# A graph network on one core: VectorE makes all selection matrices of a tile before the layer norm of the preceding tile

## What is computed

```python
x = layernorm(x + x @ W)              # W: 256 x 256, edge weights set at (src, dst)
X = x
for l in range(4):
    h   = einsum('ni,rio->rno', X, weights[l])          # 4 relations
    msg = h[etype, src] * inv_deg[:, None]
    agg = segment_sum(msg, dst)
    out = agg + X @ roots[l] + biases[l]
    X   = elu(layernorm(out) * gamma[l] + beta[l]) + X
out = layernorm(x + X)
```

## Time and profile before

| | before |
|---|---|
| median of three executions | 2757.57 us |
| profiled execution, device time | 2755.74 us |
| its span on the core | 2754.0 us |
| mean granted clock of PE | 0.814 |
| PE busy (matmuls) | 2166.8 us, 79% |
| DVE busy | 1636.5 us, 59% |
| GpSimd busy | 1515.0 us, 55% |
| ScalarE busy | 371.2 us, 13% |
| L464 PE, aggregation matmuls (two per visit) | 3712, 1269.6 us busy |
| L276 GpSimd, gathers | 1568, 1507.3 us busy |
| L919 DVE, selection matrices | 1856, 609.8 us busy |
| L373 PE, products | 800, 419.7 us busy |

### The profile page before, as it was taken

One profiled execution on the slowest core, in us unless ns is written; L12 is line 12 of the kernel. 1 busy time (PEld: TensorE's weight loads), 2 busy tenths in 40 slices (PEclk: granted clock), 3 DMA queues, 4 the chain that ended last, 5 costly groups with the idle time before them and its releaser, 6 DMA issues.

```text
span 2754.0 us, 45427 instructions
## 1 busy us (share of the span) xinstructions
PE 2166.8 (79%) x7689; PEld 1300.0 (47%) x7690; DVE 1636.5 (59%) x5784; ACT 371.2 (13%) x765; POOL 1515.0 (55%) x1591
## 2 busy tenths in 40 slices
PE   1667976777988888788888897988888868877665
PEld 0345444666544555433445564344455534444543
DVE  3988249788544567523455674345566624457677
ACT  0554320232000111100001110000011100000000
POOL 1000033000777777477777774777777567777772
PEclk9888985899778899956789997577899965667787
DMA  4000241000334444333344442334444343334341
GB/s 154 3 0 0 107 159 42 0 0 0 105 113 128 135 143 151 105 105 105 120 127 144 143 152 90 105 113 128 127 143 149 122 143 105 105 105 120 104 121 49
DMA packets 103156, 280.46 MB, mean 102 GB/s; under 512 B 27612, under 2 KB 38986, under 8 KB 102734
## 3 DMA queue, kind: packets, MB, share of 16 engines
q0 software_dynamic: 75264, 205.62, 25.5%
q10 hardware_dynamic: 17878, 62.19, 5.9%
q1 hardware_dynamic: 9848, 10.82, 1.3%
HBM read 219.61 MB, written 58.91 MB: 101 GB/s over the span
## 4 chain that ended last, share of the span: by engine, by line
PE 44%; DVE 15%; issue 13%; DMA 10%; POOL 10%; DVEq 4%; ACT 1%; POOLq 1%; SPq 1%; ACTq 0%
PE acc L464 25%; POOL ring L276 10%; DMA ring<-h_rows,idx 9%; PE hp L373 7%; PE pw L373 6%; DVE S L896 2%; PE acc L455 2%; DVE ring L746 1%; DVE hot_s L869 1%; DVE hot_n L869 1%; PE pw L349 1%; DVE S L919 1%; PE tr L362 1%; ACT XT L499 1%; POOLq L185 1%
## 5 line engine op out<-in xcount | busy, mean ns | idle before, releaser
L276 POOL DMA_INDIRECT ring<-h_rows,idx x1568 | 1507.3, 961 | 1189.2 <-issue 906.7
L464 PE MATMUL acc<-ring,S 128*128 x3712 | 1269.6, 477 | 250.9 <-SPq L229 137.3
L464 PEld LDWEIGHTS acc<-ring,S 128*128 128x128 f32 x3712 | 752.0, 225 | 744.8 <-issue 673.9
L919 DVE TENSOR_SCALAR S<-iota,ecol 128x128 f32<-128x128 f32 x1856 | 609.8, 370 | 791.0 <-PE acc L464 696.3
L373 PE MATMUL hp<-wts,XT 128*128 (+1 forms) x416 | 215.1, 665 | 22.4 <-ACT XT L499 22.4
L373 PE MATMUL pw<-wts,XT 128*128 (+1 forms) x384 | 204.6, 682 | 20.3 <-ACT XT L499 20.3
L869 DVE TENSOR_TENSOR hot_s<-iota,place 128x400 bf16<-128x400 f32 x196 | 112.4, 574 | 99.4 <-PE acc L416 84.7
L557 ACT ACTIVATE work<-work 128x256 f32<-128x256 f32 x100 | 41.7, 417 | 942.1 <-DVE work L949 931.6
L455 PE MATMUL acc<-wts,XT 128*128 (+1 forms) x400 | 122.5, 434 | 45.9 <-issue 39.2
L373 PEld LDWEIGHTS hp<-wts,XT 128*128 128x128 f32 x416 | 84.4, 214 | 122.3 <-issue 122.3
L373 PEld LDWEIGHTS pw<-wts,XT 128*128 128x128 f32 x384 | 80.1, 220 | 116.3 <-issue 116.3
(11 more groups left out here) (213 smaller groups left out, 1398.6 us busy)
## 6 DMA issues: line engine op xcount, KB each, us to landing
h_rows<-hst ACTq DMA_DIRECT2D x100, 512.0 KB
ring<-h_rows,idx POOLq DMA_INDIRECT x1568, 2.7
wts<-weights SPq DMA_DIRECT2D x32, 128.0 KB, 2.7
x_rows<-X ACTq DMA_DIRECT2D x1, 3200.0 KB, 10.1
wts<-x_rows ACTq DMA_DIRECT2D x1, 3200.0 KB, 12.6
X<-x SPq DMA_DIRECT2D x1, 3072.0 KB
out<-X ACTq DMA_DIRECT2D x2, 1024.0 KB
wts<-roots SPq DMA_DIRECT2D x8, 128.0 KB, 2.9
```

Of the source, the lines that this page charges most:

```text
L276: pool.indirect_dma_start(ring[:, k, :], None, h_gather, bass.IndirectOffsetOnAxis(ap=idx[:, g * J + j:g * J + j + 1], axis=0)).then_inc(l ...
L464: nc.tensor.matmul(accs[t % 2][:, 0:D], S[:, at * J + j, :], ring[:, bass.ds((c + j) % SLOTS, 1), :].rearrange("p a d -> p (a d)"), start= ...
L919: v.tensor_scalar(S[:, at * J + j, :], iota[:, t * P:(t + 1) * P], dst_c[:, bass.ds(c + j, 1)], inv_c[:, bass.ds(c + j, 1)], ALU.is_equal, ...
```

## The change

In the loop over the tiles, in layers 0 to 2 and in the last layer alike, the call of `weigh_rest(t)` is moved ahead of the layer norm of tile t-1. Nothing else is changed.

```diff
@@ -963,9 +963,9 @@
                 for t in range(NT):
                     visits = tile_visits(dve, t)
                     weigh_first(t, visits, lm)
+                    weigh_rest(t, visits, lm)
                     if t > 0:
                         layer_norm_elu(l, t - 1, lm + tile_end(t - 1), features(t - 1))
-                    weigh_rest(t, visits, lm)
                 layer_norm_elu(l, NT - 1, lm + tile_end(NT - 1), features(NT - 1))
 
             lm = entry(dve, T_LM + L - 1, 0, MAXV)
```

## The result

The changed kernel takes 3139.24 us (median of four executions, 3138.51 to 3142.49) where the one before takes 2756.26 in the same comparison: a ratio of 1.139, 95% interval 1.137 to 1.141, +383 us. The forecast was 3044 us, +286, with a range up to 3140: the direction and the kind of loss are right, the size is a quarter too small, and the result lies at the very end of the range (one of the four executions, 3142.49 us, lies beyond it).

What follows compares the result with a forecast made beforehand. Gathers were taken to set a layer's early pace, gathers and PE about equally late from tile 11. Bare norms and slowed clock add 88.6 us a layer, 266 for three, plus 20 in the last: +286, 3044 us, range 2940 to 3140.

Steps and rivals of the forecast that it cites:

- The bound before: Old kernel's narrow tiles from 11 on: gathers and PE about equally late, 11.85 us a tile, PE slack 1.1 us.
- the gate four visits back: DVE's late matrices: each waits for the visit four before it, so the norm of t-1 starts after visit n-4.
- the bare norm: Narrow tiles, layers one to three: of the 5.69 us norm, 4.8 to 4.9 us leave PE idle.
- the wait at the transposes: PE's transposes (L362) wait for the norm some 54 times, near 4.8 us each, 240 to 260 us in all.
- Tiles 1 to 6: Wide tiles of a layer: gathers still set the pace, 139 us of work under 169.8, so no loss.
- Four visits cover 1.8 - 0.9: Narrow tiles, first three layers: visits 9 to 12 on PE cover 0.9 us of the norm.
- the sum without the clock: Rival, clock holds: 10.2 us plus 0.45 per visit a tile, 169 us for three layers, 2947 us total; chance 0.17.
- I take 1.8: First three layers: the bare norm brings half clock rate, costing some 1.8 us in each tile.
- The other row, products after slow work: Alternative clock cost: eight product matmuls take 5.89 us after slow work against 3.67 at full clock, 2.2 us.
- The rival in which the clock returns only after the products: First three layers: all eight products at half rate lose 3.5 us a tile, 3136 us total; chance 0.16.
- 14.2 us a tile: Last layer, 13 tiles: norm, sum and statistics, eight visits with four slow, 14.2 us against 13.15, +14 in all.
- 0 to +30: Last layer: allowance in the range for how soon its clock recovers, 0 to +30 us.

Runs made afterwards that it cites:

- f2_twelve_before: Kernel before, its order kept, with twelve places for selection matrices instead of eight and no gated loop in tiles 11 to 24: 2751.11 us, ratio 0.998.
- f4_sums_later: Kernel before, with the last layer's sum and statistics of tile t-1 moved behind the late matrices of t: 2751.77 us, ratio 0.9982.
- f1_twelve_after: Changed kernel with twelve places for selection matrices instead of eight and no gated loop in tiles 11 to 24: 2763.19 us, ratio 1.0025 to the kernel before.
- e4_warm: Changed kernel plus ten unread matmuls on PE ahead of the norm wait, tiles 7 to 24 of layers 0 to 2: 3016.13 us, ratio 1.092 to before.
- e3_loads_early: Changed kernel, last layer's three register loads for tile t+1 moved ahead of the norm of t-1: 3150.68 us, ratio 1.141 to the kernel before.
- f3_loads_in_wait: Changed kernel, last layer's register loads for tile t+1 put between the first eight and the gated matrices of t: 3109.76 us, ratio 1.128 to before.

## Why the prediction was right, and where its sizes were off

**The bound before.** That the gathers set the pace and PE has about 1 us of slack in a narrow tile holds: twelve places (f2_twelve_before) and later sums (f4_sums_later) take waits away and gain only 6 us each, and where the gathers have got ahead (f1_twelve_after) a narrow tile takes 10.6 us instead of 11.85.

**The mechanism.** Right: the gate four visits back, the bare norm, the wait at the transposes. In the 54 tiles of the sum PE's idle time is 4.7 to 5.4 us, 5.05 on average, where the sum had 4.8 to 4.9. f1_twelve_after shows it from the other side. I expected such waits in some 54 tiles and 240 to 260 us. Those 54 make 273 us; with small ones in the wide tiles (1 to 3 us each) and the three at the layers' ends, as before, there are 75 and 311.3 us.

**Tiles 1 to 6.** Right, they cost nothing.

**"Four visits cover 1.8 - 0.9".** Nearly: from the last matrix to L940 it takes 0.55 us, where I had 0.25 for a register load. The cycle at full clock is 15.8 us (e4_warm, 205.7 us for 13 tiles) instead of 15.6. The +256 of e4_warm less the last layer's 71 leave 185 us, where the sum without the clock had 169. That is 16 us of the missing 97, of which 0.2 us in 54 tiles make some 12.

**The term that was mis-sized in the first three layers: "I take 1.8" for the clock.** It measures 2.35 us a tile (e4_warm), 30 us in all. The 1.8 came from four visits in the last layer, chosen for the length of idle. The other row, products after slow visits (2.2), had the right kind of work and was the better neighbour. The Trainium skill, "TensorE: Matmul & The Clock Gate" (HAM oscillation), has the mechanism, a price paid at every burst after a long enough wait, and here the trace agrees: 6.53 us after an idle of 5.23, 3.67 when the gap is filled. The rival in which the clock returns only after the products named 3136 us, near the result, but its step is not what happened: it asked for 3.5 us in every tile and got 2.35. Only in tiles like the one shown do nearly all eight products run slow; on average they lose 2.2 us.

**The step that failed in the last layer: 14.2 us a tile.** It is 17.0. Of the 2.8, 1.7 are register loads: I let DVE go from the norm to the next tile's matrices as it goes to the late matrices of the same tile before the change (0.25 us), and overlooked that `tile_visits` is then in between (e3_loads_early, f3_loads_in_wait). I had written that of a moved step everything is to be counted, and counted only what was moved, not what it was moved next to. Another 0.75 are the clock: of the eight visits on the chain I took four as slow, 5.58 us, and they take 6.3, as if some six were. The remaining 0.3 are the way from the last matrix to the norm, as in the first three layers. Over 17 tiles these are 29, 13 and 5 us, 47 of the missing 51. By stretches, tiles 8 to 10 lose 7 us where I had nothing, tiles 11 to 23 lose 54.5 where I had 14, and the layer's end 9.4 where I had 5.5. The "0 to +30" that I allowed for this layer's clock had no room for the loads.

**The range** held the result by less than 1 us. That is luck: its upper end came from the rival with the late clock, whose step did not happen, and not from the terms that were off. The first three layers' error (46 us) and the last one's (51) had the same sign, and the range had room for one of them.

**Signs named beforehand.** The clock of tiles 11 to 23 fell to 0.81 (forecast 0.85); their length was 235 (226). The norm starts 0.6 us before the end of PE's visits (forecast 0.9). In the first three layers PE's waits for gathers are gone outside tiles 0 to 6, as forecast. GpSimd's waits for PE grew by 117 us, not 200: in the second layer it is held back for the first time at 1690, and at 1787 it has issued its last gather, 112 us before the layer's end. Instead it waits longer for the next layer's rows, 105 us where before it was 31.

## What to carry to other kernels

Count what a move makes neighbours: the work that loses its cover, and also the small things (register loads, a loop's exit) that used to sit in somebody's wait and now sit on the chain. Work gated by "a few steps back" ties a producer to its consumer, so whatever is queued behind it starts late however early it stands in the code; more places loosen it (f1_twelve_after), another order does not. And a stall of one engine has a length, it lowers the clock of the work after it, and it gives the slower engine of the pipeline time to get ahead, which may pay it back in full (f1_twelve_after).

## What the runs showed of the hardware

Three register loads from SBUF cost DVE 1.7 to 1.9 us between two instructions, as much as six selection matrices. Adding ten matmuls a tile (4.48 us each time) to PE made the changed kernel 127 us faster, since it kept the granted clock at 1.00. After some 5 us of idle the products took 5.70 us on average to the next root products, and 6.37 in the tile shown, instead of 3.51; in that tile the clock was back only for the root products, in most within the products.
